# Low halves of a split product moved from VectorE to GpSimd in a fused RWKV and mixture-of-experts kernel

## The reference

```
x = x + tanh(g_xattn) * wkv(time_decay, time_first, k=layernorm(x), v=ctx)   # a recurrence over the 256 steps
z = layernorm(x)
shared = (silu(z @ W_gate) * (z @ W_up)) @ W_down                            # 512 -> 2 x 1408 -> 512
routed = top 2 of 8 experts, each (silu(z @ U_gate) * (z @ U_up)) @ U_down   # 512 -> 2 x 352 -> 512, capacity 1280
x = x + tanh(g_ffn) * (routed + shared)
```

## Time and profile before

| | |
|---|---|
| median of 3 runs | 1355.05 us (1352.57 to 1355.46) |
| the profiled execution | 1355.17 us |
| its span, first to last instruction | 1353.4 us |
| busy in the span: TensorE matmul, VectorE, ScalarE, GpSimd | 1269.2, 835.5, 582.6, 553.8 us |
| mean granted TensorE clock | 0.986 |
| low half L1173 on VectorE | 176 times, 143.6 us |

### The profile page before, as it was taken

How to read it: one execution, slowest core, us unless ns; L and a number is a source line. 1 busy time by engine, 2 the same in 40 slices (tenths; PEclk the granted TensorE clock), 3 DMA queues, 4 the chain that set the end, 5 groups by cost and what they waited for, 6 DMA issues and landing times. The chain is left out here.

```text
span 1353.4 us, 27909 instructions
## 1 busy us (share of the span) xinstructions
PE 1269.2 (94%) x9861; PEld 973.2 (72%) x9861; DVE 835.5 (62%) x1655; ACT 582.6 (43%) x1102; POOL 553.8 (41%) x600
## 2 busy tenths in 40 slices
PE   1579999999999999999998869999999999999999
PEld 1467777777777777777767747777777777877854
DVE  6787888788797888888977434343434344334212
ACT  5665435344344444353443324444444444444320
POOL 7874343352352433433533213444434443443420
PEclk9999999999999999999999879999999999999999
DMA  9261222112121212121201325555646555655447
GB/s 240 59 202 40 71 48 63 56 47 55 55 70 55 55 55 70 47 59 59 64 17 32 70 77 111 109 120 114 130 100 133 113 118 119 123 107 110 88 68 274
DMA packets 103690, 121.95 MB, mean 90 GB/s; under 512 B 43102, under 2 KB 66678, under 8 KB 103457
## 3 DMA queue, kind: packets, MB, share of 16 engines
q1 hardware_dynamic: 82688, 78.40, 20.3%
q0 software_dynamic: 20064, 42.19, 17.3%
q10 hardware_dynamic: 832, 0.02, 0.0%
HBM read 72.19 MB, written 46.81 MB: 88 GB/s over the span
## 5 line engine op out<-in xcount | busy, mean ns | idle before, releaser
L899 PE MATMUL PU<-xT,wreg 128*128 128x256 f16 x4224 | 503.2, 276 | 10.8 <-DMA xT<-wkv 8.1
L899 PEld LDWEIGHTS PU<-xT,wreg 128*128 128x128 f16 x4224 | 414.0, 99 | 85.6 <-issue 12.8
L913 PE MATMUL PD<-wreg,hreg 128*128 128x512 f16 x858 | 206.4, 379 | 0.0
L600 POOL DMA_INDIRECT moe_d<-acc x80 | 126.8, 1584 | 113.1 <-ACT acc L787 96.2
L986 PE MATMUL PU<-acc,wkv 128*128 128x256 f16 (+1 forms) x1440 | 163.7, 276 | 4.2 <-DVE acc L1327 4.0
L986 PEld LDWEIGHTS PU<-acc,wkv 128*128 128x128 f16 (+1 forms) x1440 | 147.7, 107 | 21.8 <-issue 5.7
L986 PE MATMUL PU<-acc 128*128 128x256 f16 (+1 forms) x1440 | 160.5, 273 | 0.0
L986 PEld LDWEIGHTS PU<-acc 128*128 128x128 f16 (+1 forms) x1440 | 146.6, 106 | 15.4 <-issue 0.2
L1336 DVE SCALAR_TENSOR_TENSOR acc<-PU,acc 128x256 f32<-128x256 f32 (+1 forms) x120 | 50.8, 423 | 167.2 <-ACT acc L778 167.1
L706 ACT ACTIVATE hreg<-srng 128x256 f16<-128x256 f32 x176 | 72.3, 411 | 178.6 <-DVE srng L1166 177.8
L1173 DVE TENSOR_TENSOR hreg<-srng,hreg 128x256 f16<-128x256 f32 x176 | 143.6, 816 | 0.1
(11 more groups left out here) (146 smaller groups left out, 1613.9 us busy)
## 6 DMA issues: line engine op xcount, KB each, us to landing
wkv<-in_L_ffn_w_up_gate SPq DMA_DIRECT2D x64, 176.0 KB, 3.7
acc<-in_x SPq DMA_DIRECT2D x32, 256.0 KB, 3.1
wkv<-in_ctx SPq DMA_DIRECT2D x32, 256.0 KB, 2.7
xln_d<-wkv SPq DMA_DIRECT2D x32, 256.0 KB, 2.3
moe_d<-acc SPq DMA_DIRECT2D x13, 512.0 KB, 2.9
out<-moe_d SPq DMA_DIRECT2D x2, 3328.0 KB, 21.2
acc<-n_L_ffn_shared_w_up_gate SPq DMA_DIRECT2D x16, 256.0 KB, 5.9
wkv<-in_L_ffn_w_down SPq DMA_DIRECT2D x16, 256.0 KB, 4.7
```

Of the source, the lines that this page charges most:

```text
L600: pool.indirect_dma_start(out=moe_d, out_offset=bass.IndirectOffsetOnAxis(ap=eidx[:, p, 1, s:s + 1], axis=0), in_=ostage[s % 2], in_offset ...
L899: mm = pe.matmul(PU[r][:, gu * UN:(gu + 1) * UN], sU[:, m, gu, a, kt, :], xT[:, u.par, b, kt, :], start=(kt == 0 and a + b == 0), stop=(kt ...
L913: mm = pe.matmul(PD[t][:, :], hh[:, u.par, j, a, t * P:(t + 1) * P], sD[:, j, b, :], start=(j == 0 and a + b == 0), stop=(j == JT - 1 and ...
```

## The change

The low half of the units 0 to 14 is made by GpSimd instead of VectorE: 165 of 176. GpSimd makes it first in each of its steps, two steps behind the tile as before; the last two of unit 14 stand behind its loop, in front of the last sends of slots. The low halves of unit 15 stay on VectorE, and there VectorE waits until GpSimd's are counted, because `hlo_ready` is one counter. Nothing is changed on ScalarE, TensorE and SyncE.

```diff
@@ gpsimd
+            def hidden_lo(u, m):
+                n = JT * u.v + m
+                r = m % SP_N
+                pool.wait_ge(hhi_ready, n + 1)
+                pool.tensor_tensor(hh[:, u.par, m, 1, :], srng[:, r, :], hh[:, u.par, m, 0, :], ALU.subtract).then_inc(hlo_ready, 1)
+
             def unit(u, first=0):
                 for s in range(first, JT):
+                    if not (u.fixed and u.v < 0):
+                        w = u if s >= 2 else u.shift(-1)
+                        if w.exists():
+                            hidden_lo(w, (s - 2) % JT)
                     for v, k in tiles_at("factors", u, s):
                         factors(v.tile(k))
...
             for v in range(2 * LOOP[1], UNITS - 1):
                 unit(Unit(0, v))
+            for m in (JT - 2, JT - 1):
+                hidden_lo(Unit(0, UNITS - 2), m)
             for r in LAST:
@@ vector
             def hidden_lo(u, m, buf):
                 n = JT * u.v + m
                 r = m % SP_N
+                dve.wait_ge(hlo_ready, n)
                 dve.wait_ge(hhi_ready, n + 1)
...
-            def buf_of(u):
-                return 2 if u.fixed and u.v == UNITS - 1 else u.par
-
             def unit(u, first=0, also=None):
                 for s in range(first, JT):
                     if not (u.fixed and u.v < 0):
-                        for m in (s - 1, s - 2):
-                            work = hidden if m == s - 1 else hidden_lo
-                            w = u if m >= 0 else u.shift(-1)
-                            if w.exists():
-                                args = (w, m % JT) if m == s - 1 else (w, m % JT, buf_of(w))
-                                work(*args)
+                        w = u if s > 0 else u.shift(-1)
+                        if w.exists():
+                            hidden(w, (s - 1) % JT)
+                        if u.fixed and u.v == UNITS - 1 and s >= 2:
+                            hidden_lo(u, s - 2, 2)
```

## The result

The changed kernel takes 1339.38 us (median of 5 runs, 1338.4 to 1339.82) against 1355.05 us (1352.57 to 1355.46): a ratio of 0.989, 95% interval 0.9876 to 0.9903. The profiled span fell by 15.3 us, from 1353.4 to 1338.1.

The account below looks back on a forecast made before the run. TensorE was taken to bound the kernel except in two stretches, elements 0 and 14, where it waits and VectorE comes last. Gains of 2.4 + 3.4 = 5.8 us off 1355.2 gave 1349.4 us, range 1345.5 to 1356.

Parts of the forecast that it names:

- The low half costs GpSimd 0.66 us: Each of 165 added GpSimd subtractions of 128x256 was taken at 0.66 us, with bounds of 0.42 and 1.18.
- sum 2.4 us: Element 0, 58.9 to 99.6 us: gain of 1.0 where nmr ends plus 1.4 from there to the division's end.
- `nmr` end at 86.0: Element 0, step 7: GpSimd's mean and deviation end 1.0 us earlier than the 87.0 of before.
- 3.4 us: Elements 13 to 15: the split of 743.85 and the transpose behind it come 3.4 us earlier.
- some 0.5: Element 14: GpSimd's mean and deviation (nmr) come only some 0.5 us earlier, read off the order of instructions.
- VectorE's 508 us there cost nothing: Elements 1 to 13, 99.6 to 706.6 us: TensorE is busy 603.95 of 607.00 us, so VectorE's work costs nothing.
- the long stretch keeps its 46.7 us for an element: Sign expected in the profile after: elements 1 to 13 still take 46.7 us each.
- a shorter wait can also return some clock: Matmuls behind TensorE's wait at 708.79 ran at granted clock 0.94; a shorter wait can return clock, no size given.
- (a): Rival: all of VectorE's relief arrives, 6.9 us in element 0, about 4.5 at the end: 11 us, 1344; chance 0.10.
- (b): Rival: 16 two-input VectorE instructions in two elements meet GpSimd's low halves, 5.3 us eat the gain: 1354.7; chance 0.20.
- (c): Rival: silu starves behind GpSimd's late low halves, 12 us lost in six even elements: 1361; chance 0.10 for over 0.2% loss.
- point of decision at 8 us of lateness: The silu rival decides once a low half is late by more than some 8 us; the prediction found 3.3.

Follow-up runs that it names:

- x_mid: The changed kernel's move limited to elements 1 to 12, all other low halves on VectorE as in the kernel before: 1349.03 us, ratio 0.9954.
- b_lo_behind_div: The kernel before, all low halves on VectorE, but in steps 4 and 10 of elements 0 to 14 made behind the division: 1346.87 us, ratio 0.9945.
- a_lo_last: The changed kernel with the low half last instead of first in each of GpSimd's steps: 1352.95 us, ratio 0.9991 to the kernel before.

## Why the prediction was wrong, point by point

**Right.** The low half costs GpSimd 0.66 us: between 100 and 700 us its minimum, median and maximum are

```profile
L530 POOL TENSOR_TENSOR hreg<-srng,hreg x142: 659/670/1652, 106.4 to 699.5; 128x256 f16<-128x256 f32 x142
```

Element 0, in its mechanism: "sum 2.4 us", measured 3.03 at the turn, or 3.74 from where element 0 began. Its step is visible on GpSimd, where the prediction had `nmr` end at 86.0 (before 87.0):

```profile
85.75 0.26 POOL L479 TENSOR_SCALAR nmr<-mv,rstd 128x1 f32<-128x1 f32 x1 [0.21 <-POOL rstd L477]
```

Behind it the division's product ended at 96.55 and met a GpSimd instruction once more:

```profile
95.15 1.40 DVE L1146 TENSOR_TENSOR wkv<-wkv 128x512 f32<-128x512 f32 x1
```

That is 3.03 us before 99.58, by the prediction's order of causes; the part from `nmr` to there, 1.4 in the sum, is 2.0. Elements 13 to 15: "3.4 us", measured 3.56 from the end of the long stretch to the start of element 15. GpSimd's part in it was read rightly too: `nmr` of element 14 ends 11.27 us behind TensorE's arrival at the turn, before 11.57, so 0.3 sooner; the prediction had "some 0.5".

**Wrong, first step: "VectorE's 508 us there cost nothing", and "the long stretch keeps its 46.7 us for an element".** The stretch held 4.62 us that the change gave back (B), and an element takes 46.0 us now. The earlier trace rows said so: TensorE was busy 603.95 of 607.00 us. The 3.05 us of idle time were read as none, though they were half of the whole forecast. The chain was the one of the two turns that the prediction did look at, low half, reciprocal, product, transposes; at five turns inside the stretch it was late by some tenths of a microsecond, and each cost 0.9 us. x_mid shows the same 4.6 with GpSimd's low halves in this stretch alone, b_lo_behind_div with the low half behind the division.

**Wrong, second step: "a shorter wait can also return some clock" had no term.** At the first turn it was the difference between 5.01 and 2.78 us for 24 matmuls and between 1.11 and 0.66 for the transposes, in sum 5.74 - 3.03 = 2.71 us, nearly as much as the 3.03 us by which the turn came earlier. The earlier trace rows had the other such row, 4.45 us; what it would be at full speed stood in any row of the long stretch (2.78). At the turn to element 14 it returned 1.67 us more, but there nothing of it lasted: at the logits of element 14 the changed kernel was 10.45 us ahead (715.05, wait 3.62, against 725.50, wait 0.65), as it had been ahead of the turn. At element 15, 9 matmuls took 1.14 instead of 2.08 us, 0.94 us of D; yet the six kernels with 1.14 have D from 601.2 to 604.5 (mean 602.5), the five with 2.08 from 602.9 to 604.8 (mean 604.1). The means lie the right way apart, the ranges overlap: whether the 0.94 us last to the end is open.

So the sum of the prediction, 2.4 + 3.4, stands against 3.03 + 3.56; 4.62 and 2.71 had no term, and 1.38 in D is within the scatter. That is also why the start of element 15 came 13.9 us earlier and not 5.8.

**The rivals.** (a) gave a number near by, 1344, for another reason: all low halves of element 0 and of the end were to count. (b), the lock, exists but is small. Two-input instructions of VectorE between 100 and 700 us in the changed kernel (busy, mean ns):

```profile
L1138 DVE TENSOR_TENSOR_SCAN wkv<-wkv 128x516 f32<-128x516 f32 x26 | 39.9, 1534 | 0.9
...
L1160 DVE TENSOR_TENSOR wkv<-wkv 128x512 f16<-128x512 f32 x26 | 23.4, 900 | 0.0
```

They had means of 1242 and 719 ns: 26 x 0.29 + 26 x 0.18 = 12.3 us went back to them of the 122.7 us that the low halves had taken there. They aren't all: the 26 small copies of L1171 take 11.4 us instead of 4.4, and with the other groups some 26 us came back in B. VectorE has room in that stretch. (c), silu behind GpSimd, is no cost of this change (B has none), but it is near. With the low half last in the step instead of first the kernel takes 13.6 us more, and 9.5 of them go with a fourth slot (B and C); with each made twice B is 13.0 us longer, where TensorE's main wait is another, behind `nmr` (8.1 us). The prediction had its point of decision at 8 us of lateness; the longest wait of silu was 5.3 us in the changed kernel and 6.6 in a_lo_last, which already cost.

## What to carry to other kernels

A stretch in which the bounding engine is busy 99.5% still holds the other 0.5%: in 600 us that is 3 us, and a wait of 0.5 us names the chain that is late. Look at what stands in front of the late result on its engine before moving work to another engine: here one subtraction made behind the division instead of in front of it, twice an element, gave 7.6 us, half of what the change gave, with every engine keeping its instructions. Its own duration fell with the move, from 1.31 to 0.42 us in element 4, because it no longer met GpSimd's addition. And price a wait of TensorE with the matmuls behind it, by the same row in an undisturbed place.

## What the runs showed of the hardware

The 24 matmuls of 256 columns behind a wait take 2.78 us at a granted clock of 1.00 (96.61 to 99.92 in the changed kernel). Where they take 5.01 and 4.45 (kernel before) and 3.73 (b_lo_behind_div), the stretches 99.64 to 105.66, 709.48 to 713.76 and 99.83 to 104.56 have 0.52, 0.60 and 0.67. Waits in front of the transposes and the duration of the 24 behind, over the kernels: 0.28, 0.57, 0.62, 0.94, 1.70, 1.78 and 1.93 us: 2.78 each time; 2.13: 4.30; 2.14: 4.45; 2.42: 3.73; 2.53: 4.45; 3.00: 5.02; 3.92: 5.01. It isn't the length of the wait alone: in x_mid one of 2.68 us before the logits at 721.01 was followed by 2.78, in the changed kernel one of 3.62 at 715.05 by 4.45. What decides beyond the wait is not shown. In a_lo_last the turn to element 1 was 0.34 us earlier than in the changed kernel (96.27), behind a wait of 3.00 us, and A was 2.37 us later: an earlier result behind a longer wait can lose. Of TensorE's two levels, 1.00 is the upper, 2.4 GHz.

A copy of 128x2 elements on VectorE took 1.47 us beside GpSimd's work in element 14, in the changed kernel:

```profile
703.81 1.47 DVE L1171 COPY topv<-top 128x2 f32<-128x2 f32 x1
```

The 32 such copies of the whole execution average 483 ns after and 195 ns before. It has one SBUF input. The Trainium skill (SBUF — State Buffer, Who interferes with whom) says that copies can enter a mode in which they take the port pair that GpSimd uses, and that the other side is then blocked for a whole instruction; the trace agrees in that the copy began in GpSimd's multiplication of 703.21 (1.04 us) and ended at 705.28, with the next one (704.21 to 705.24): it sat out two instructions. That this copy was in such a mode no run shows.
